# A hybrid state-space layer on one core: the slice softmax in two halves, square sums on GpSimd, and a reordered transpose loop in the last graph layer

## The chip, the cores and the metric

The kernel runs on one core of a Trainium2 chip, as one launch. The metric is the device time of that core in microseconds (us), the median of several runs. The core has five engines that run their own instruction streams in program order and meet through semaphores: TensorE (PE; its weight loads are shown apart as PEld), VectorE (DVE), ScalarE (ACT), GpSimd (POOL) and SyncE (SP), which only issues DMAs here. Matmul results land in PSUM; all other tiles lie in SBUF, 128 partitions wide.

## The reference, cut to what matters

The network has four layers on `x` of shape (128, 40, 128), float32; each layer adds a graph network and a feed-forward network to `x`. Two of these eight blocks are touched.

The feed-forward block of layer 0 assigns the 40 nodes of each graph to 64 slices per head, runs a bidirectional state-space mixer over the slices, and returns to the nodes. Its parts that matter here:

```
w    = softmax(logits / temperature)        # (graph, node, 8 heads, 64 slices)
norm = sum of w over the nodes              # 1 / (norm + 1e-5) scales the slice tokens
...                                         # projection, convolution, scan, gate
yg = yg * rsqrt(mean(yg * yg, -1) + 1e-5) * norm_w      # 512 features
return yg @ out_w.T                         # then back to the nodes with w
```

The graph block of layer 3 is an attention with 8 heads of 40 x 40:

```
logits = q + swapaxes(k, -1, -2)
masked = leaky_relu(logits + (1 - adj) * NEG)
attn   = softmax(masked, axis=-1)
out    = attn @ feat_proj                   # then a projection, a residual, a sigmoid
```

## The kernel before

**Layer 0, feed-forward (`l0_ffn`).** The 128 graphs go in 16 chunks of 8 graphs (`NCH = 16`), each of 4 groups of 2 graphs (`CHP = 4`); of a pair of graphs, one lies on partitions 0 to 39 and the other on 64 to 103. The work is a software pipeline over turns `c = -2 .. 15` (`all_turns`). In one turn each engine does a part of chunk c+2 (logits and softmax), a part of chunk c+1 (slice tokens, input projection, convolution) and the end of chunk c (mixing, gate, norm, output projection, return to the nodes). The order on each engine is written out by hand in its `turn` function, and every engine does exactly what stands there, in that order. A turn on TensorE is: `slices` and `input_projection` of c+1, `mix` of c (L3601), `steps_down` of c+1 (L3571), `logits` of c+2 (L3507, L3508), `gains` of c+1 (L3581, L3583), then

- `output_projection` of group 0 (L3620, 8 matmul records), which waits for the gate (`yg1`),
- `squares` (L3609): four one-column matmuls that average the squared features over the partitions; it waits for `sq_sum`,
- `output_projection` of groups 1 and 2; group q from 2 on waits until ScalarE has copied group q-2 out of the same PSUM bank (`ot_out`),
- `slice_sums` of c+2 (L3519), which waits for the finished softmax (`smd`),
- `output_projection` of group 3, `back_to_nodes` (L3632), `transposed(0)` and `(1)`, `dt_down`, `to_features` (L3642).

The copy of an output group on ScalarE (`out_copy`, L3763) scales by `rms`, which comes from the squares by a chain: Square on ScalarE (L3748), two adds on VectorE that fold four feature blocks into one (`square_sums`, L3897 over 1024 elements and L3899 over 512), `squares` on TensorE, a square root on ScalarE (`root`, L3752), a reciprocal on VectorE (`scales`, L3903).

The softmax of chunk c+2 works in place on the tile `sw` of 128 x 2048 (4 groups of 8 heads of 64 slices). VectorE adds biases to four groups as their logits arrive (`biases`, L3793 into `sw`, L3794 into `fx`), then runs `square_sums(c)`, then the maximum (L3801), the subtraction (L3803, `smx`), `scales(c)`, a wait for one Exp over the whole tile on ScalarE (L3684, `sme`), the sum (L3806), a reciprocal (L3808) and the product (L3810, `smd`). `inverses` (L3815) waits for `slice_sums` of TensorE. Behind it on VectorE stand two pieces of work for a later layer (`kept.piece`, L2481 to L2491), copies for the return (L3908), `out` (L3913), and the states of the next turn (L3827).

On ScalarE a turn ends with `squares`, `root`, `exps(c + 2)`, four `out_copy` and `nodes`. Exp and Sqrt use different tables, so a table load stands before each.

GpSimd has one job in this block: `kept.fetch`, which moves 32 pieces (two in a turn) of an edge list through two buffers: an iota, a wait until VectorE has made the piece (`done`), two DMAs out, a wait for them, and two DMAs in for the piece after the next. All of it stands in one loop.

In the last turns nothing of chunks c+2 or c+1 is left: turn 14 has no logits and no softmax, turn 15 only `mix`, the gate, `squares`, the output projection and the return.

**Layer 3, graph (`l3_gnn`).** 16 chunks of 4 pairs, 64 pairs in all. For each pair TensorE turns the 8 heads of both graphs (16 matmuls of 40 x 40 against the identity, L2279, 32 records), ScalarE copies them to `PT` (L2327), TensorE multiplies them with the features (L2242), ScalarE copies that to `Z` (L2301), and once in a chunk 8 projections follow (L2252), spread over the next chunk's pairs 1 to 3. Graph j = 0 of a pair uses rows and output partitions 0 to 39, j = 1 uses 64 to 103, and each has a PSUM bank of its own. The loop runs over j outside and over the 8 heads inside:

```
for j in range(2):
    for h in range(HD):
        mm = pe.matmul(pst[n % 2][j][rows(j), h, :], P[rows(j), c % 2, h, q, :], g.ident[...], ...)
```

VectorE makes the softmax of the next chunk (L2372 to L2384) around an Exp on ScalarE (L2311), and the sigmoid's end of an earlier one (L2389 to L2400); the first of these waits for the projections. GpSimd adds keys, queries and masks (L2348, L2353: 1280 elements a partition each). The graph block of layer 2 has a similar transpose (L1974), whose loop runs over pairs outside and j inside, 8 matmuls with 16 records in a chunk.

Of the kernel before, what the change touches and what calls it, by code (L numbers as in the profile page):

```python
# [19 lines left out]
NCH = B // CHG  # L20
# [2137 lines left out]
def l3_gnn(nc, g):  # L2158
# [4 lines left out]
    with nc.cleanup_on_exit(), ExitStack() as ctx:  # L2163
# [54 lines left out]
        def _(pe):  # L2218
# [52 lines left out]
            for c in range(NCH):  # L2271
                pe.wait_ge(attn, c + 1)
                for q in range(CHP):
                    n = c * CHP + q
                    if n >= 2:
                        pe.wait_ge(pt_out, n - 1)
                    for j in range(2):
                        for h in range(HD):
                            mm = pe.matmul(pst[n % 2][j][rows(j), h, :], P[rows(j), c % 2, h, q, :], g.ident[rows(j), rows(j)], start=True, stop=True)  # L2279
                    mm.then_inc(pt_ps, 1)  # L2280
                    if q == 1 and c >= 1:
                        project(c - 1, HEADS_AT[q])
                    if n >= 1:
                        product(n - 1)
                    if c < NCH - 3 and q >= 2:
                        query(c + 3, 2 * q - 4)
                        query(c + 3, 2 * q - 3)
                    if q >= 2 and c >= 1:
                        project(c - 1, HEADS_AT[q])
# [143 lines left out]
class EdgeKeys:  # L2433
# [22 lines left out]
    def fetch(self, pool):  # L2456
        W = self.WIDTH
        ends = [self.g.L2_ffn_edge_index[i].rearrange("(p c) -> p c", p=128) for i in range(2)]

        def load(i):  # L2460
            pool.dma_start(self.src[:, i % 2], ends[0][:, i * W:(i + 1) * W]).then_inc(self.ld[i % 2], 16)
            pool.dma_start(self.dst[:, i % 2], ends[1][:, i * W:(i + 1) * W]).then_inc(self.ld[i % 2], 16)

        load(0)
        load(1)
        for i in range(self.PIECES):
            pool.iota(self.place[:], pattern=[[-1, W]], base=-WIDE - i * W % WIDE, channel_multiplier=0, allow_small_or_imprecise_dtypes=True).then_inc(self.io, 1)
            pool.wait_ge(self.done, i + 1)
            pool.dma_start(self.w_dram[:, i * W:(i + 1) * W], self.src[:, i % 2]).then_inc(self.st[i % 2], 16)  # L2469
            pool.dma_start(self.k_dram[:, i * W:(i + 1) * W], self.dst[:, i % 2].bitcast(F32)).then_inc(self.st[i % 2], 16)  # L2470
            if i + 2 < self.PIECES:
                pool.wait_ge(self.st[i % 2], 32 * (i // 2 + 1))
                load(i + 2)
# [741 lines left out]
def l0_ffn(nc, g, kept, sorted_rows):  # L3215


    with nc.cleanup_on_exit(), ExitStack() as ctx:
# [14 lines left out]
        with ExitStack() as first:  # L3233
# [121 lines left out]
            def _(dve):  # L3355
# [22 lines left out]
                for par in range(2):  # L3378
# [29 lines left out]
                                 "g_ps", "w_rdy", "y_ps", "yg1", "sq", "sq_sum", "r_ps", "rt", "rms", "ot_ps", "ot_out", "o_ps", "oT_out", "oT_act", "f_ps", "f_out", "init", "settled")}  # L3408
# [27 lines left out]
        @block.gpsimd  # L3436
        def _(pool):
            sorted_rows.fill(pool, g.x)
            kept.fetch(pool)
# [50 lines left out]
        def _(pe):  # L3490
# [19 lines left out]
            def slice_sums(k):  # L3510

                pe.wait_ge(s["smd"], k + 1)
# [132 lines left out]
            def turn(c, par):  # L3645
# [13 lines left out]
                if there(c):  # L3659
                    output_projection(c, range(1))  # L3660
                    squares(c)
                    output_projection(c, range(1, CHP - 1))
# [15 lines left out]
        def _(act):  # L3678
# [3 lines left out]
            def exps(k):  # L3682
                act.wait_ge(s["smx"], k + 1)
                act.activation(sw[:], sw[:], ACT.Exp).then_inc(s["sme"], 1)  # L3684
# [80 lines left out]
            def turn(c, par):  # L3765
# [5 lines left out]
                if there(c):  # L3771
                    squares(c)
                    root(c)
                if there(c + 2):
                    exps(c + 2)
# [7 lines left out]
        def _(dve):  # L3783
# [5 lines left out]
            def biases(k):  # L3789

                for q in range(CHP):
# [3 lines left out]
                dve.drain()  # L3795

            def softmax(k, meanwhile):

                sw3 = sw[:].rearrange("p q (h n) -> p (q h) n", n=SG)
                bc = sst[:, :, None].broadcast_to([128, CHP * SH_, SG])  # L3800
                dve.tensor_reduce(sst[:], sw3, AX.X, ALU.max)  # L3801
                dve.drain()
                dve.tensor_tensor(sw3, sw3, bc, ALU.subtract).then_inc(s["smx"], 1)  # L3803
                meanwhile()
                dve.wait_ge(s["sme"], k + 1)
                dve.tensor_reduce(sst[:], sw3, AX.X, ALU.add)  # L3806
                dve.drain()
                dve.reciprocal(sst[:], sst[:])  # L3808
                dve.drain()
                dve.tensor_tensor(sw3, sw3, bc, ALU.mult).then_inc(s["smd"], 1)  # L3810
# [84 lines left out]
            def square_sums(k):  # L3895
                dve.wait_ge(s["sq"], k + 1)
                dve.tensor_tensor(sq[:, 0:2], sq[:, 0:2], sq[:, 2:4], ALU.add)  # L3897
                dve.drain()
                dve.tensor_tensor(sq[:, 0], sq[:, 0], sq[:, 1], ALU.add).then_inc(s["sq_sum"], 1)  # L3899

# [28 lines left out]
            def turn(c, par):  # L3929
# [16 lines left out]
                if there(c + 2):  # L3946
                    biases(c + 2)
                if there(c):
                    square_sums(c)
                if there(c + 2):  # L3950
                    softmax(c + 2, lambda: scales(c) if there(c) else None)
                    inverses(c + 2)
                else:
                    scales(c)
# [135 lines left out]
```

## Time and profile before

| what | us |
|---|---|
| runs before: median (lowest, highest) of 3 | 3103.75 (3088.63, 3108.38) |
| the profiled execution | 3108.4 |
| its span from first to last instruction | 3106.7 |
| TensorE busy | 2448.8 (79%) |
| VectorE busy | 2092.8 (67%) |
| ScalarE busy | 1311.9 (42%) |
| GpSimd busy | 729.9 (23%) |

The page of the profile gives these shares, the span in 40 slices of 77.7 us, the costliest groups of instructions and what ended the idle time before them. A timeline view gives instructions in order of time; a run of like instructions is merged into one row. A windows view gives busy times, the number of instructions and the granted TensorE clock (1.00 is the higher of its two levels, 0.50 the lower) in a stretch. Ends of matmuls are modelled, so starts are the safer numbers on TensorE.

### The profile page before, as it was taken

What the parts mean: (1) busy time and instruction counts of PE and PEld (TensorE: products, weight loads), DVE (VectorE), ACT (ScalarE), POOL (GpSimd) and SP (SyncE); (2) the same over time, 40 slices, a digit from 0 to 9 for tenths busy, and PEclk for the clock granted to TensorE, in tenths of its full rate; (3) what the DMA queues carried; (4) which work ended last, traced back from release to release, by engine and by line L of the source; (5) the groups of instructions that cost most, each with busy time, mean ns of one, the idle gap of its engine ahead of it and who ended that gap; (6) DMA issues with size and microseconds to landing.
All of it is one profiled execution on the core that took longest, in us unless ns stands there. A gap on an engine that the chain in (4) does not pass through costs nothing. (4 is left out here: it accounts for less than half of the span.)

```text
span 3106.7 us, 50319 instructions
## 1 busy us (share of the span) xinstructions
PE 2448.8 (79%) x18840; PEld 1551.7 (50%) x18840; DVE 2092.8 (67%) x4114; ACT 1311.9 (42%) x2407; POOL 729.9 (23%) x756
## 2 busy tenths in 40 slices
PE   6467999999999999996567566868758989996291
PEld 5334555545555444553436555634424666664291
DVE  6846888888888878886666797766673356775132
ACT  4334444444444444442457403333214454555171
POOL 0000000000000000001007582047730013440666
PEclk7778999999999999998768857579978997887596
DMA  4341222212222211221323412000012221111263
GB/s 81 114 128 29 53 55 56 55 49 55 56 55 56 56 49 44 57 52 56 101 68 93 79 42 36 8 10 6 6 17 60 68 49 36 44 35 35 75 177 102
DMA packets 189057, 178.78 MB, mean 58 GB/s; under 512 B 83700, under 2 KB 162176, under 8 KB 185976
## 3 DMA queue, kind: packets, MB, share of 16 engines
q1 hardware_dynamic: 168064, 137.00, 17.6%
q0 software_dynamic: 20768, 38.75, 5.2%
q8 instruction: 145, 2.38, 0.3%
q14 instruction: 80, 0.66, 0.1%
HBM read 139.11 MB, written 43.64 MB: 59 GB/s over the span
## 5 line engine op out<-in xcount | busy, mean ns | idle before, releaser
L3557 PE MATMUL hy_ps<-hy_uT,hy_win 128*128 128x512 f32 x1152 | 501.4, 596 | 0.0
L3557 PEld LDWEIGHTS hy_ps<-hy_uT,hy_win 128*128 128x128 f32 x1152 | 218.9, 191 | 286.3 <-issue 286.3
L2469 POOL DMA_DIRECT2D ek_w<-ek_src x32 | 17.8, 556 | 1128.2 <-DVE ek_dst L2491 1128.2
L3620 PE MATMUL hy_ps<-hy_wo,hy_yg 128*128 128x512 f32 x512 | 236.7, 607 | 22.3 <-ACT XNP L3763 15.5
L3055 PE MATMUL er_c<-XNG 128*128 128x400 f32 x480 | 181.0, 534 | 0.0
L3620 PEld LDWEIGHTS hy_ps<-hy_wo,hy_yg 128*128 128x128 f32 x512 | 93.2, 191 | 131.5 <-issue 97.5
L3842 DVE TENSOR_TENSOR_SCAN XNG<-XNG,hy_fx 128x2048 f32<-128x2048 f32 x32 | 141.6, 4425 | 3.0 <-issue 0.4
L2988 POOL DMA_INDIRECT er_gone<-er_nodes,er_sidx x120 | 125.3, 1044 | 36.6 <-issue 35.6
L3055 PEld LDWEIGHTS er_c<-XNG 128*128 128x128 f32 x480 | 95.7, 205 | 68.8 <-issue 12.6
L946 DVE TENSOR_TENSOR f_hg<-f_hs,f_gb 128x640 f32<-128x640 f32 x64 | 52.7, 825 | 110.1 <-ACT f_hs L928 91.3
L2252 PE MATMUL g_ps<-g_Z,g_wc 128*128 128x320 f32 x256 | 106.5, 564 | 1.1 <-ACT g_Z L2301 1.1
L3693 ACT ACTIVATE hy_swT<-hy_ps 64x160 f32<-64x160 f32 x256 | 76.4, 299 | 72.7 <-PE hy_ps L3524 67.9
L2690 PE MATMUL f_px<-XNG 128*128 128x40 bf16 x736 | 69.2, 266 | 47.9 <-DVE XNG L2605 46.7
L1724 POOL DMA_INDIRECT XNP<-f_y,f_pidx x80 | 96.5, 1206 | 42.2 <-issue 24.1
L3793 DVE TENSOR_TENSOR hy_sw<-hy_ps,hy_blg 128x512 f32<-128x512 f32 x64 | 44.3, 692 | 91.2 <-PE hy_ps L3508 91.2
L2279 PEld LDWEIGHTS g_ps<-ident,g_P 40*40 40x40 f32 x2048 | 83.5, 128 | 44.5 <-issue 36.9
L928 ACT ACTIVATE f_hs<-f_ph,f_b1t 128x320 f32<-128x320 f32 x128 | 67.0, 527 | 84.5 <-PE f_ph L896 83.9
L2279 PE MATMUL g_ps<-ident,g_P 40*40 40x40 f32 x2048 | 91.2, 215 | 12.3 <-DVE g_obias L2414 9.5
L3712 ACT ACTIVATE hy_xr<-hy_ps 128x512 f32<-128x512 f32 x80 | 47.9, 599 | 123.9 <-PE hy_ps L3557 123.5
L1710 POOL DMA_INDIRECT f_xg<-f_xn,f_gidx x94 | 91.1, 969 | 28.7 <-issue 27.5
L3763 ACT ACTIVATE XNP<-hy_ps,hy_rms 128x512 f32<-128x512 f32 x64 | 42.2, 682 | 129.2 <-PE hy_ps L3620 128.6
L2690 PEld LDWEIGHTS f_px<-XNG 128*128 128x128 bf16 x736 | 60.7, 152 | 56.4 <-DVE XNG L2605 56.4
(698 smaller groups left out, 5944.7 us busy)
## 6 DMA issues: line engine op xcount, KB each, us to landing
XNG<-hy_decays SPq DMA_DIRECT2D x32, 1024.0 KB, 10.4
hy_rb<-hy_inverse SPq DMA_DIRECT2D x128, 128.0 KB, 3.5
f_gb<-gate_rows SPq DMA_DIRECT2D x16, 640.0 KB, 5.1
g_KB<-g_keys SPq DMA_DIRECT2D x32, 320.0 KB
f_xg<-f_rows SPq DMA_DIRECT2D x54, 128.0 KB
f_ys<-f_ysl SPq DMA_DIRECT2D x54, 128.0 KB
f_y<-f_ysl SPq DMA_DIRECT2D x47, 128.0 KB
f_rows<-in_x_dram POOLq DMA_DIRECT2D x2, 2560.0 KB, 15.6
```

The costliest lines, as they stand in the source:

```text
L928: ins = act.activation(hs[:, e % 2, k, :], psh[e % 2][k][:], ACT.Gelu, bias=b1t[:, e * H2 + k:e * H2 + k + 1])
L1710: pool.indirect_dma_start(out=xg[:, i % NX, h, :], out_offset=None, in_=ex.xn_dram, in_offset=bass.IndirectOffsetOnAxis(ap=ex.gidx[:, n:n ...
L1724: pool.indirect_dma_start(out=yc[:, n % NC_, t, c, :], out_offset=None, in_=ex.y_dram, in_offset=bass.IndirectOffsetOnAxis(ap=ex.pidx[:, n ...
L2252: mm = pe.matmul(psy, wc[:, h, :], Z[:, c % 2, h].rearrange("p b n -> p (b n)"), start=(h == 0), stop=(h == HD - 1))
L2279: mm = pe.matmul(pst[n % 2][j][rows(j), h, :], P[rows(j), c % 2, h, q, :], g.ident[rows(j), rows(j)], start=True, stop=True)
L2690: mm = pe.matmul(self.ph, self.OL[:, b, :, k], self.OH[:, b, :, k], start=False, stop=False, skip_group_check=True)
L2988: pool.indirect_dma_start(out=gone[:, par, u, :], out_offset=None, in_=tab_dram, in_offset=bass.IndirectOffsetOnAxis(ap=sidx[:, par, u:u + ...
L3055: mm = pe.matmul(flat(acc[j][:]), OD[:, 1 - par, u, j * 128:(j + 1) * 128], flat(X[:, u]), start=False, stop=False, skip_group_check=True)
L3557: mm = pe.matmul(p[:], win[:, t, m * 128:(m + 1) * 128], uT[:, t, :], start=(t == 0), stop=(t == KT - 1))
L3620: mm = pe.matmul(PS[4 + q % 2][:], yg[:, t, q * 128:(q + 1) * 128], wo[:, t, :], start=(t == 0), stop=(t == KT - 1))
L3693: ins = act.activation(o, p[:, :, j, 0:N], ACT.Copy)
L3842: dve.tensor_tensor_scan(L[:, a][:, st], dAb[:, a][:, st], E[:, st], 0.0, ALU.mult, ALU.add)
```

## The change

Layer 0: the softmax of a chunk is done in two halves of two groups each. VectorE makes biases, maximum and subtraction of groups 0 and 1, then of groups 2 and 3 (`shifted`), then `scales(c)`, then sum, reciprocal and product of each half (`scaled`). ScalarE runs Exp on the first half, then the root of chunk c, then Exp on the second half. The two adds of the squares move from VectorE to GpSimd. On TensorE `squares(c)` moves in front of the output projection, whose groups 0 to 2 follow it in one stretch. GpSimd's loop over the pieces is opened: the same steps as before, with the square sums of a chunk ahead of its two pieces. `slice_sums` waits for both halves.

Layer 3: the transpose loop runs over heads outside and j inside.

```diff
-                    for j in range(2):
-                        for h in range(HD):
+                    for h in range(HD):
+                        for j in range(2):
                             mm = pe.matmul(pst[n % 2][j][rows(j), h, :], P[rows(j), c % 2, h, q, :], g.ident[rows(j), rows(j)], start=True, stop=True)
...
         def _(pool):
+            def square_sums(k):
+                pool.wait_ge(s["sq"], k + 1)
+                pool.tensor_tensor(sq[:, 0:2], sq[:, 0:2], sq[:, 2:4], ALU.add).then_inc(s["sq_half"], 1)
+                pool.wait_ge(s["sq_half"], k + 1)
+                pool.tensor_tensor(sq[:, 0], sq[:, 0], sq[:, 1], ALU.add).then_inc(s["sq_sum"], 1)
+
             sorted_rows.fill(pool, g.x)
-            kept.fetch(pool)
+            kept.fetch(pool, 0)
+            kept.fetch(pool, 1)
+            for c in range(NCH):
+                square_sums(c)
+                kept.keep(pool, 2 * c)
+                kept.refill(pool, 2 * c)
+                kept.keep(pool, 2 * c + 1)
+                kept.refill(pool, 2 * c + 1)
...
-                pe.wait_ge(s["smd"], k + 1)
+                pe.wait_ge(s["smd"], 2 * k + 2)
...
                 if there(c):
-                    output_projection(c, range(1))
                     squares(c)
-                    output_projection(c, range(1, CHP - 1))
+                    output_projection(c, range(CHP - 1))
                 if there(c + 2):
                     slice_sums(c + 2)
...
-            def exps(k):
-                act.wait_ge(s["smx"], k + 1)
-                act.activation(sw[:], sw[:], ACT.Exp).then_inc(s["sme"], 1)
+            def exps(k, f):
+                act.wait_ge(s["smx"], 2 * k + f + 1)
+                act.activation(sw[:, 2 * f:2 * f + 2], sw[:, 2 * f:2 * f + 2], ACT.Exp).then_inc(s["sme"], 1)
...
                     squares(c)
+                if there(c + 2):
+                    exps(c + 2, 0)
+                if there(c):
                     root(c)
                 if there(c + 2):
-                    exps(c + 2)
+                    exps(c + 2, 1)
...
+            def shifted(k, f):
+
+                for q in range(2 * f, 2 * f + 2):
                     dve.wait_ge(s["lf_ps"], 4 * k + q + 1)
                     dve.tensor_tensor(sw[:, q, :], PS[q % 2][:], blg[:], ALU.add)
                     dve.tensor_tensor(fx[:, q, :], PS[2 + q % 2][:], bfx[:], ALU.add).then_inc(s["lg_out"], 1)
                 dve.drain()
+                sw3, part, wide = half_of(f)
+                dve.tensor_reduce(part, sw3, AX.X, ALU.max)
+                dve.drain()
+                dve.tensor_tensor(sw3, sw3, wide, ALU.subtract).then_inc(s["smx"], 1)
+
+            def scaled(k, f):
+
+                dve.wait_ge(s["sme"], 2 * k + f + 1)
+                sw3, part, wide = half_of(f)
+                dve.tensor_reduce(part, sw3, AX.X, ALU.add)
+                dve.drain()
+                dve.reciprocal(part, part)
+                dve.drain()
+                dve.tensor_tensor(sw3, sw3, wide, ALU.mult).then_inc(s["smd"], 1)
...
                 if there(c + 2):
-                    biases(c + 2)
+                    shifted(c + 2, 0)
+                    shifted(c + 2, 1)
                 if there(c):
-                    square_sums(c)
+                    scales(c)
                 if there(c + 2):
-                    softmax(c + 2, lambda: scales(c) if there(c) else None)
+                    scaled(c + 2, 0)
+                    scaled(c + 2, 1)
                     inverses(c + 2)
-                else:
-                    scales(c)
```

## Rows read from the trace of the kernel before

**Rows 1.** Windows view: layer 0 feed-forward between its ends; layer 3 graph
```profile
core 0: us, PE busy (x) PEld busy (x) DVE busy (x) ACT busy (x) POOL busy (x), PEclk, DMA share, GB/s
...
255.00:1397.00 1142.00, 1066.71 (x9282) 568.91 (x9282) 918.15 (x1183) 543.24 (x949) 67.98 (x140) 0.99 0.21 52
...
2567.00:2824.00 257.00, 253.89 (x2648) 172.08 (x2648) 174.48 (x160) 128.41 (x284) 89.82 (x28) 0.82 0.14 35
```
**Rows 2.** Timeline of PE, one turn (start us, us, instruction [idle before <-releaser])
```profile
708.91 3.68 PE L3620 MATMUL hy_ps<-hy_wo,hy_yg 128*128 128x512 f32 x8
...
713.23 3.68 PE L3620 MATMUL hy_ps<-hy_wo,hy_yg 128*128 128x512 f32 x8
717.99 3.70 PE L3620 MATMUL hy_ps<-hy_wo,hy_yg 128*128 128x512 f32 x8 [1.08 <-ACT XNP L3763]
722.53 1.08 PE L3519 MATMUL hy_ps<-hy_sw,hy_selS 128*32 128x128 f32 x32 [0.84 <-DVE hy_sw L3810]
...
737.88 1.92 PE L3560 MATMUL hy_ps<-hy_uT,hy_wdt 128*40 128x512 f32 x8 [1.84 <-DVE hy_uT L3827]
```
**Rows 3.** Timeline of DVE, the same turn
```profile
704.66 0.68 DVE L3794 TENSOR_TENSOR hy_fx<-hy_ps,hy_bfx 128x512 f32<-128x512 f32 x1
...
708.87 1.22 DVE L3897 TENSOR_TENSOR hy_uT<-hy_uT 128x1024 f32<-128x1024 f32 x1
...
710.78 2.28 DVE L3801 TENSOR_REDUCE hy_sst<-hy_sw 128x32 f32<-128x2048 f32 x1
...
717.40 2.29 DVE L3806 TENSOR_REDUCE hy_sst<-hy_sw 128x32 f32<-128x2048 f32 x1 [1.89 <-ACT hy_sw L3684]
...
720.18 2.29 DVE L3810 TENSOR_TENSOR hy_sw<-hy_sw,hy_sst 128x2048 f32<-128x2048 f32 x1
```
**Rows 4.** Timeline of ACT, the same turn
```profile
701.55 1.92 ACT L3748 ACTIVATE hy_uT<-hy_yg 128x2048 f32<-128x2048 f32 x1
...
713.69 1.28 ACT L3684 ACT_TABLE_LOAD   x1
715.46 1.91 ACT L3684 ACTIVATE hy_sw<-hy_sw 128x2048 f32<-128x2048 f32 x1 [0.48 <-DVE hy_sw L3803]
```
**Rows 5.** Tile views of layer 3's keys and attention (min/median/max ns)
```profile
L2348 POOL TENSOR_TENSOR g_KB<-g_KB,g_Q x16: 2390/2392/2397, 2550.9 to 2782.7; 128x1280 f32<-128x1280 f32 x16
L2353 POOL TENSOR_TENSOR g_KB<-g_KB,a_adjG x16: 2882/4024/4032, 2553.3 to 2785.2; 128x1280 f32<-128x1280 f32 x16
...
L2378 DVE TENSOR_TENSOR g_P<-g_P,g_st x16: 1491/2257/2264, 2559.4 to 2798.4; 128x1280 f32<-128x1280 f32 x16
```
**Rows 6.** Timeline of PE: first softmax, and the last two turns
```profile
182.97 1.93 PE L3519 MATMUL hy_ps<-hy_sw,hy_selS 128*32 128x128 f32 x32 [13.28 <-DVE hy_sw L3810]
...
1398.22 3.70 PE L3620 MATMUL hy_ps<-hy_wo,hy_yg 128*128 128x512 f32 x8
...
1402.56 10.55 PE L3620 MATMUL hy_ps<-hy_wo,hy_yg 128*128 128x512 f32 x24
...
1442.37 5.30 PE L3620 MATMUL hy_ps<-hy_wo,hy_yg 128*128 128x512 f32 x8 [6.80 <-DVE hy_yg L3892]
```
**Rows 7.** Timeline of ACT, turn 14: the Square
```profile
1397.29 1.92 ACT L3748 ACTIVATE hy_uT<-hy_yg 128x2048 f32<-128x2048 f32 x1
```
**Rows 8.** Timeline of PE: turned heads in layer 2, and twice in layer 3
```profile
1939.83 0.50 PE L1974 MATMUL g_t<-ident,g_P 40*40 40x40 f32 x16
...
2649.25 1.29 PE L2279 MATMUL g_ps<-ident,g_P 40*40 40x40 f32 x32 [0.44 <-DVE g_P L2384]
...
2687.20 2.11 PE L2279 MATMUL g_ps<-ident,g_P 40*40 40x40 f32 x32
```
**Rows 9.** Timeline of DVE in layer 3: the same step of two successive chunks
```profile
2635.22 0.55 DVE L2389 SCALAR_TENSOR_TENSOR g_so<-g_ps,g_obias,XNP 128x320 f32<-128x320 f32 x1 [0.34 <-PE g_ps L2252]
...
2649.11 0.55 DVE L2389 SCALAR_TENSOR_TENSOR g_so<-g_ps,g_obias,XNP 128x320 f32<-128x320 f32 x1
```
**Rows 10.** Windows view: one chunk of layer 3, mostly at the low clock
```profile
2581.00:2603.00 22.00, 21.88 (x170) 14.68 (x171) 8.63 (x8) 7.67 (x17) 6.40 (x2) 0.58 0.13 31
```

More of the change, by code:

```diff
@@ L2454, in hold, with fetch, keep, refill @@
         self.ld = [sem(f"ld{b}") for b in range(2)]
-    def fetch(self, pool):
+    def fetch(self, pool, i):
         W = self.WIDTH
[L2458 to L2473, printed above, removed]
+        cols = slice(i * W, (i + 1) * W)
+        for t, end in ((self.src, 0), (self.dst, 1)):
+            rows_ = self.g.L2_ffn_edge_index[end].rearrange("(p c) -> p c", p=128)
+            pool.dma_start(t[:, i % 2], rows_[:, cols]).then_inc(self.ld[i % 2], 16)
+    def keep(self, pool, i):
+        W = self.WIDTH
+        pool.iota(self.place[:], pattern=[[-1, W]], base=-WIDE - i * W % WIDE, channel_multiplier=0, allow_small_or_imprecise_dtypes=True).then_inc(self.io, 1)
+        pool.wait_ge(self.done, i + 1)
+        pool.dma_start(self.w_dram[:, i * W:(i + 1) * W], self.src[:, i % 2]).then_inc(self.st[i % 2], 16)
+        pool.dma_start(self.k_dram[:, i * W:(i + 1) * W], self.dst[:, i % 2].bitcast(F32)).then_inc(self.st[i % 2], 16)
+    def refill(self, pool, i):
+        if i + 2 < self.PIECES:
+            pool.wait_ge(self.st[i % 2], 32 * (i // 2 + 1))
+            self.fetch(pool, i + 2)
     def piece(self, dve, i):
@@ L3407, in l0_ffn @@
                                  "ip_ps", "ip_out", "dt_half", "dt_sum", "cv", "xs", "dtln", "dt_rdy", "da_exp", "da_rdy", "da_ld", "xt_ps", "xt_out",
-                                 "g_ps", "w_rdy", "y_ps", "yg1", "sq", "sq_sum", "r_ps", "rt", "rms", "ot_ps", "ot_out", "o_ps", "oT_out", "oT_act", "f_ps", "f_out", "init", "settled")}
+                                 "g_ps", "w_rdy", "y_ps", "yg1", "sq", "sq_half", "sq_sum", "r_ps", "rt", "rms", "ot_ps", "ot_out", "o_ps", "oT_out", "oT_act", "f_ps", "f_out", "init", "settled")}
         da_st = [sem(f"da_st{i}") for i in range(2)]
@@ L3787, in _, with half_of @@
             dve.nop().then_inc(s["f_out"], 2)
-            def biases(k):
-                for q in range(CHP):
+            def half_of(f):
+                part = sst[:, f * 2 * SH_:(f + 1) * 2 * SH_]
+                return sw[:, 2 * f:2 * f + 2].rearrange("p q (h n) -> p (q h) n", n=SG), part, part[:, :, None].broadcast_to([128, 2 * SH_, SG])
+            def shifted(k, f):
+                for q in range(2 * f, 2 * f + 2):
                     dve.wait_ge(s["lf_ps"], 4 * k + q + 1)
@@ L3795, in biases @@
                 dve.drain()
[L3797 to L3801, printed above, removed]
+                sw3, part, wide = half_of(f)
+                dve.tensor_reduce(part, sw3, AX.X, ALU.max)
                 dve.drain()
[L3803 to L3806, printed above, removed]
+                dve.tensor_tensor(sw3, sw3, wide, ALU.subtract).then_inc(s["smx"], 1)
[3 more added lines that the diff above has]
+                dve.tensor_reduce(part, sw3, AX.X, ALU.add)
                 dve.drain()
-                dve.reciprocal(sst[:], sst[:])
+                dve.reciprocal(part, part)
                 dve.drain()
-                dve.tensor_tensor(sw3, sw3, bc, ALU.mult).then_inc(s["smd"], 1)
+                dve.tensor_tensor(sw3, sw3, wide, ALU.mult).then_inc(s["smd"], 1)
             def inverses(k):
@@ L3893, in gate @@
                 ins.then_inc(s["yg1"], 1)
[L3895 to L3899, printed above, removed]
             def scales(k):
```

## The prediction

> **What bounds the kernel now.** I read the windows view by stage first, then the timelines of the engines through one turn. In the inner part of layer 0's feed-forward block TensorE is busy for 1066.71 of 1142 us at a granted clock of 0.99, VectorE for 918.15 [rows 1]. So TensorE sets the end there, and an edit pays only if it takes away one of TensorE's waits. In layer 3's graph block TensorE is busy for 253.89 of 257 us, at a clock of 0.82, VectorE for 174.48 [rows 1]: TensorE again, but with a clock that comes and goes.
>
> The timeline of one turn shows where TensorE waits in the stretch that the change rewrites. An output group of 8 records lasts 3.68 us alone and three in a row last 10.55 [rows 2, 6], so an unhindered group puts off its successor by (10.55 - 3.68) / 2 = 3.43 us. From group 1 to group 2 there are 717.99 - 713.23 = 4.76 us: 1.33 too many, spent on the copy of group 0, which waits for the root. From group 2 to the slice sums there are 722.53 - 717.99 = 4.54: 1.11 too many, spent on the softmax [rows 2]. The idle figures at those rows, 1.08 and 0.84, are smaller because modelled ends overlap the next start; I go by starts. That is 2.44 us in a turn. Both waits need a softmax and square sums in the same turn, which turns 0 to 13 have: 14 turns, 34.2 us.
>
> **Do both waits go?** I lay out the turn of rows 2 to 4 anew. TensorE reaches the squares at 708.91, where group 0 starts now. Group 0, squares and the start of group 1 take 4.32 us, so the squares take 0.89; then group 0 starts at 709.8, group 1 at 713.2, group 2 at 716.7, and the slice sums could start at 720.1.
>
> *Square sums on GpSimd.* Square ends on ScalarE at 701.55 + 1.92 = 703.5 [rows 4]. No row shows such an add on GpSimd here; the nearest are its adds of 1280 elements: 2.39 with a broadcast operand, 2.88 at the least and 4.02 in the median with a full one [rows 5]. For 1024 plus 512 elements, 1.2 times as many, that is 2.9 to 4.8 us. I take 3.5, from the 2.88, since these operands are full. The sums are ready at 707.0, at the latest 708.3, and TensorE wants them at 708.9: no wait. The queue in front on GpSimd is last turn's pieces, and GpSimd is busy for 67.98 of 1142 us [rows 1]. Behind the new wait stand the iota and the DMAs of this turn's pieces; VectorE wants them only after the slice sums, some 13 us later. All of the pieces' DMAs keep their number and their distance to the piece that releases them. SP's queue isn't touched.
>
> The add's 2.88 became 4.02 where a subtraction of VectorE with two SBUF operands ran beside it, and that subtraction went from 1.49 to 2.26 [rows 5]: one waits for the other. The Trainium skill, "SBUF — State Buffer", section "SBUF: two separate sides", says that the two engines hold a shared port exclusively for a whole instruction, which speaks against an add on GpSimd beside a softmax. By that rule the first half's subtraction waits for the end of the second add, at most about half a microsecond, and the sum stays as it is; the trace agrees in size.
>
> *Softmax in halves.* The second operation of group 1 ends at 705.34, unchanged [rows 3]. An operation over 1024 elements costs 1.22 us [rows 3] and 0.08 for the drain; half of the 2.29 of a full one, 1.15, is the lower bound. Maximum and subtraction of the first half end at 707.9. Groups 2 and 3 are four operations of 0.68: 710.7. Their maximum and subtraction: 713.3, and the reciprocal of the root, a short one: 713.5. Each half then needs a sum, a reciprocal with its drains and a product: 1.22 + 0.49 + 1.22 = 2.9, where 0.49 is the gap from 717.40 + 2.29 to 720.18 [rows 3]. The second product ends at 719.4 instead of 722.47. What went: 1.9 us of adds from 708.87 to 710.78, and the 1.89 of waiting for Exp [rows 3]; half an Exp now runs beside the other half's work. TensorE comes at 720.1, so the margin is 0.7 us, or 1.5 with the lower bound, or 0.2 if the port costs half a microsecond. Each tenth that is missed costs 1.4 us in 14 turns.
>
> *Root between the Exps.* ScalarE pays a table load more in each turn, 1.28 us [rows 4]. First Exp: 707.9 to 708.9 (half of 1.91). Table: 710.2. Root, whose squares are done at 709.9: 710.5. Table: 711.8. It then waits for the second half until 713.3 anyway, so the load is hidden. Second Exp: 714.3; copy of group 0 until 715.0. Group 2 needs that copy at 716.7: 1.7 us to spare, and beyond these the load would cost its own length.
>
> Everything behind the slice sums (inverses, their DMAs, the pieces, states) hangs on them or on TensorE's later work, so the ring follows as a whole: a turn of 34.2 / 14 = 2.44 us less.
>
> **The ends of the pipeline.** The first two turns have a softmax and nothing beside it; TensorE waits 13.28 us for the first [rows 6]. The wait for Exp goes there too: 2 x 1.9 = 3.8 us won. Turn 14 has no logits that cover the squares: Square ends at 1399.21 [rows 7], GpSimd at 1402.7, and TensorE stands from 1398.22 [rows 6], where it now does group 0: 4.5 us lost. In turn 15 the gate ends at 1442.3, Square takes 1.9 and GpSimd 3.5, so the squares start at 1447.8. Today group 0 runs beneath that (5.3 us at the low clock [rows 6]); it then comes after: 5.5 us lost, bounds 3.4 and 7. Layer 0: 34.2 + 3.8 - 4.5 - 5.5 = 28 us won.
>
> **The loop in layer 3.** 16 records with j inside last 0.50 us in layer 2, 32 with j outside last 1.29 [rows 8], both at the high clock. If records of the two graphs overlap, 32 cost some 0.78 (0.50 and 16 more at 0.28), so 0.5 us in each of 64 groups: 32 us at most at the high clock. Against this stands VectorE: its step L2389 comes 13.89 us after the one before in a chunk in which it hardly waits (0.34), and TensorE then waits for it (0.44) [rows 8, 9]. A chunk can't fall below 13.9, and the mean is 257 / 16 = 16.1 [rows 1]. The excess lies in chunks with the clock down, as the one of 22.0 at 0.58 [rows 10], where a group costs 2.11 [rows 8]. Chunks at the floor gain nothing, the others 2 us and more. I take 15 of the 32. Bounds: 30 won, and below nothing, in the rival on the clock.
>
> **The sum.** 28 + 15 = 43 us. The profiled execution took 3108.4 (span 3106.7 and 1.7 around it): 3065.4. It lies 4.65 above the median shown, so 3061 for the median.
>
> **The rivals.**
> *Layer 3 gives nothing* (VectorE's floor, or no overlap of records): for it the 0.44 wait [rows 8]; against it the 0.50 of layer 2. 28 us: 3076. The same time comes out if the halves are late and the wait for the softmax, 1.11 a turn, stays.
> *Layer 0 gives the time back.* TensorE waits 1.84 us for the states before the input projection [rows 2]; if VectorE's states don't move up, this wait grows by 2.44 and only the ends are left: 3.8 - 10 = -6, and 15 from layer 3: 3095. Against it: VectorE is released by the slice sums themselves.
> *The clock of layer 3 falls, and the whole is slower.* With shorter groups TensorE waits about 2 us in each chunk for VectorE. If that brings the low clock for the whole stage, a chunk costs the 22.0 of rows 10 less about 0.9 in each of four groups, 18.4, and 16 of them 294 us: 37 more than now, less 28 from layer 0: 3113. It decides from a mean chunk of 16.1 + 28 / 16 = 17.8 us. For it: the clock of 0.82 in a stage in which TensorE hardly waits [rows 1]; against it: in the low chunk of rows 10 TensorE is busy for 21.88 of 22.00 us, so it wasn't waiting that brought the clock down there. The Trainium skill, "TensorE: Matmul & The Clock Gate", section "HAM oscillation", warns that small gaps between groups of matmuls bring the clock down; [rows 10] show a low clock without a gap of that kind.
>
> **How the numbers follow.** Chances: forecast 0.60, layer 3 without a gain 0.20, layer 0 giving back 0.13, low clock 0.07. A measurement here can tell about 1% from no change, 31 us. The forecast lies 43 below; a part of it, and little of the first rival, falls on either side of 3073: faster 0.64, within 1% 0.33, slower 0.03. Range 3040 (all bounds good: 34 from layer 0, 30 from layer 3) to 3095 (the third case): what is left out is the low clock and some of the third.
>
> **What would show it.** A turn of 74.4 us; TensorE without idle time before groups 2 and the slice sums; L3519 about 11.2 us after the first squares; the two GpSimd adds together 3 to 4.8 us and done before TensorE comes; a new wait at L3609 in turns 14 and 15 alone. In layer 3 groups under 0.9 us at the high clock, a stage of some 242 us, more waits for L2384. Wrong: a squares wait in each turn, slice sums later than 720.1 on this scale, or L2279 groups still above 1.2 us.

## The result, and the profile after

Median 3074.64 us over 7 runs (3068.62 to 3077.12), beside 3101.85 for the kernel before over 7 runs (3084.28 to 3108.38): a ratio of 0.9919, 95% interval 0.9893 to 0.9945. That is 27 us faster, inside the range; the forecast said 43. The profiled execution took 3077.12 us (span 3075.4), 31.3 less than the one before.

The end is near; the way to it isn't the one that was forecast. Cutting both traces at the same instructions gives, in us:

| stretch | before | after | gain | forecast |
|---|---|---|---|---|
| layer 0, first logits to the last projection to features | 1301.9 | 1301.1 | 0.8 | 28 |
| layer 3's turned heads, L2279 first to last | 254.0 | 225.2 | 28.8 | 15 |
| everything else | | | 1.7 | 0 |

Layer 0, where the change has all of its parts but one, gained nothing in this pair of profiles. The 1.7 is a sum of -6.3 ahead of layer 0's block, 9.2 between the two stretches and -1.2 at the end, where nothing was edited: single profiles differ by that much. The windows view of the changed kernel, over the stretches of [rows 1]:

```profile
core 0: us, PE busy (x) PEld busy (x) DVE busy (x) ACT busy (x) POOL busy (x), PEclk, DMA share, GB/s
255.00:1397.00 1142.00, 1083.93 (x9302) 578.31 (x9303) 906.75 (x1235) 570.66 (x981) 121.74 (x171) 0.96 0.21 53
2563.00:2789.00 226.00, 206.36 (x2640) 132.00 (x2640) 173.31 (x159) 123.56 (x280) 89.86 (x28) 0.87 0.16 39
```

In layer 0 TensorE is busy for longer than before, 1083.93 us instead of 1066.71, at a granted clock of 0.96 instead of 0.99: the waits went, and slower matmuls took their place. In layer 3 it went the other way: fewer busy microseconds and a higher clock.

The turn itself came out as laid out. The timelines of all engines through a turn without a low clock, in order of time:

```profile
705.59 2.35 POOL L3440 TENSOR_TENSOR hy_uT<-hy_uT 128x1024 f32<-128x1024 f32 x1 [39.86 <-ACT hy_uT L3760]
708.02 1.27 POOL L3442 TENSOR_TENSOR hy_uT<-hy_uT 128x512 f32<-128x512 f32 x1
708.76 1.61 DVE L3818 TENSOR_TENSOR hy_sw<-hy_sw,hy_sst 128x1024 f32<-128x1024 f32 x1
710.94 1.03 PE L3622 MATMUL hy_ps<-mean_w,hy_uT 128*128 128x1 f32 x8
711.83 10.55 PE L3633 MATMUL hy_ps<-hy_wo,hy_yg 128*128 128x512 f32 x24
712.78 0.26 ACT L3764 ACTIVATE hy_rms<-hy_ps,eps 128x4 f32<-128x4 f32 x1
714.15 1.22 DVE L3818 TENSOR_TENSOR hy_sw<-hy_sw,hy_sst 128x1024 f32<-128x1024 f32 x1
719.72 1.23 DVE L3828 TENSOR_TENSOR hy_sw<-hy_sw,hy_sst 128x1024 f32<-128x1024 f32 x1
722.31 1.08 PE L3532 MATMUL hy_ps<-hy_sw,hy_selS 128*32 128x128 f32 x32
737.37 1.92 PE L3573 MATMUL hy_ps<-hy_uT,hy_wdt 128*40 128x512 f32 x8 [1.55 <-DVE hy_uT L3845]
```

The three groups of [rows 2] have become one row of 10.55 us with no wait in it or behind it. Such turns last 74.4 to 74.5 us, where those before lasted 76.4 to 77.0.

But only some turns are like that. TensorE's timeline in the next turn:

```profile
783.75 0.68 PE L3594 MATMUL hy_ps<-hy_Cs,hy_xs 64*64 64x64 f32 x16
784.36 1.06 PE L3596 MATMUL hy_ps<-hy_wfd,hy_xs 128*128 128x8 f32 x8
785.28 1.03 PE L3622 MATMUL hy_ps<-mean_w,hy_uT 128*128 128x1 f32 x8
786.17 12.24 PE L3633 MATMUL hy_ps<-hy_wo,hy_yg 128*128 128x512 f32 x24
```

The same 24 records last 12.24 us instead of 10.55. The windows view (columns as above) around the start of these groups, and of the same groups in the turn before:

```profile
712.00:715.00 3.00, 3.00 (x8) 1.33 (x8) 2.83 (x4) 2.31 (x3) 0.00 (x0) 1.00 0.00 0
782.90:786.30 3.40, 3.40 (x36) 2.57 (x35) 3.33 (x5) 1.53 (x2) 0.92 (x2) 1.00 0.03 5
786.30:789.70 3.40, 3.40 (x6) 1.34 (x6) 3.24 (x5) 2.35 (x3) 0.00 (x0) 0.51 0.00 0
```

TensorE has no idle time by its records (3.40 of 3.40), yet the clock is at 1.00, the high level of 2.4 GHz, up to the groups and at 0.51, the low one of 1.2 GHz, right behind their start. What stood ahead of the fall is a row of small matmuls: the gains (L3594, L3596) and now the squares too, 2.4 us together. A window of 3 us behind the start of the groups is well below 1.00 in 7 of the turns 0 to 13, and in none of the kernel before. Another 5 low stretches begin elsewhere in the turn, behind transposes, slices or the wait before the input projection, where TensorE did have idle time just before; before there were 3 of that kind. One stretch costs a turn about 1.75 us: turns with one last 76.0 to 76.7, which is most of what the waits had given.

The last two turns, TensorE's timeline:

```profile
1394.04 1.87 PE L3622 MATMUL hy_ps<-mean_w,hy_uT 128*128 128x1 f32 x8 [4.74 <-POOL hy_uT L3442]
1395.77 16.45 PE L3633 MATMUL hy_ps<-hy_wo,hy_yg 128*128 128x512 f32 x32
1447.18 1.86 PE L3622 MATMUL hy_ps<-mean_w,hy_uT 128*128 128x1 f32 x8 [12.43 <-POOL hy_uT L3442]
1448.90 15.48 PE L3633 MATMUL hy_ps<-hy_wo,hy_yg 128*128 128x512 f32 x32
```

Here the squares do wait for GpSimd, and behind the wait they last 1.87 instead of 1.03 and the groups 16.45 instead of about 14.0. So from the projection to features of turn 0 to that of turn 13 the trace goes from 1004.5 to 990.3 us (14.2 won, where 13 turns of 2.44 are 31.7), and from turn 13 to turn 15 from 111.8 to 128.2 (16.4 lost, where 10 were expected).

Layer 3: the timelines of TensorE and VectorE in two successive chunks, to be held against [rows 8, 9]:

```profile
2602.84 0.55 DVE L2389 SCALAR_TENSOR_TENSOR g_so<-g_ps,g_obias,XNP 128x320 f32<-128x320 f32 x1
2602.87 0.81 PE L2279 MATMUL g_ps<-ident,g_P 40*40 40x40 f32 x32
2616.73 0.55 DVE L2389 SCALAR_TENSOR_TENSOR g_so<-g_ps,g_obias,XNP 128x320 f32<-128x320 f32 x1
2616.87 0.81 PE L2279 MATMUL g_ps<-ident,g_P 40*40 40x40 f32 x32 [1.52 <-DVE g_P L2384]
```

A group of 32 records takes 0.81 us instead of 1.29, TensorE now waits 1.52 us for VectorE, and VectorE's step comes 13.89 us after the last one, the very distance of [rows 9]. The idle time before L2279 that L2384 ends rose from 8.8 us in 12 waits to 31.1 in 22; the view counts matmuls and weight loads together, and for the matmuls alone it is 2.9 us in 5 waits and 12.3 in 9.

### The profile page after: what moved, and what is told of

Read it like the earlier page. It is cut to its first block and busy times, and to the rows that moved or that the text cites. A ratio compares the mean times of both kernels' runs of the same rounds, so it can differ in the third digit from the quotient of the medians.

```text
span 3075.4 us, 50462 instructions
## 1 busy us (share of the span) xinstructions
PE 2427.9 (79%) x18840; PEld 1527.6 (50%) x18840; DVE 2073.6 (67%) x4162; ACT 1330.0 (43%) x2437; POOL 782.2 (25%) x788
## 5 line engine op out<-in xcount | busy, mean ns | idle before, releaser
L3633 PE MATMUL hy_ps<-hy_wo,hy_yg 128*128 128x512 f32 x512 | 243.3, 632 | 0.0
L3440 POOL TENSOR_TENSOR hy_uT<-hy_uT 128x1024 f32<-128x1024 f32 x16 | 37.6, 2353 | 731.1 <-ACT hy_uT L3760 731.1
L3633 PEld LDWEIGHTS hy_ps<-hy_wo,hy_yg 128*128 128x128 f32 x512 | 100.6, 201 | 121.1 <-issue 121.1
L2252 PE MATMUL g_ps<-g_Z,g_wc 128*128 128x320 f32 x256 | 95.2, 514 | 4.4 <-ACT g_Z L2301 4.4
L1390 POOL DMA_INDIRECT f_rows<-XNG,f_pidx x80 | 76.8, 960 | 48.6 <-issue 23.8
L1548 POOL DMA_INDIRECT XNP<-f_ys,f_pidx x80 | 77.7, 972 | 38.7 <-issue 23.8
```

Source lines behind the costliest of these rows:

```text
L1390: pool.indirect_dma_start(out=self.x_dram[h], out_offset=bass.IndirectOffsetOnAxis(ap=self.pidx[:, t, c:c + 1], axis=0), in_=self.xn[:, t, ...
L1548: pool.indirect_dma_start(out=yc[:, n % NC_, t, c, :], out_offset=None, in_=ex.y_dram[n // (PARTS // ex.HALVES)], in_offset=bass.IndirectO ...
L2252: mm = pe.matmul(psy, wc[:, h, :], Z[:, c % 2, h].rearrange("p b n -> p (b n)"), start=(h == 0), stop=(h == HD - 1))
L3633: mm = pe.matmul(PS[4 + q % 2][:], yg[:, t, q * 128:(q + 1) * 128], wo[:, t, :], start=(t == 0), stop=(t == KT - 1))
```

## The experiments

Two theories stood after the result. Mine: in layer 0 the squares, put right behind the gains, make one row of small matmuls behind which the clock falls, and that eats what the removed waits gave. The rival: the falls belong to the shorter turn, to halves and adds, or to whatever the chip does in a run, and the order of the squares is innocent. Each kernel ran on one chip beside runs of the kernel before, and its ratio is to those; "turns 0 to 13", "13 to 15" and "layer 3" are the stretches used above.

**Squares behind the first group again.** The changed kernel with one line moved:

```diff
 if there(c):
+    output_projection(c, range(1))
     squares(c)
-    output_projection(c, range(CHP - 1))
+    output_projection(c, range(1, CHP - 1))
```

> The changed kernel with one edit: squares(c) stands behind output group 0 again, as before the change; halves, root between the Exps, adds on GpSimd and the layer 3 loop stay. Theory (order and clock): in the changed kernel 7 of the low-clock stretches in layer 0's inner part begin right after a run of small matmuls (gains, then squares), and turns 14 and 15 wait for GpSimd with nothing beneath. With a dense group between gains and squares these 7 go (some 1.7 us each, 12 in all), and turns 13 to 15 take some 112 us from one to_features to the last instead of 128; the time falls by about 27 to 3047, with a turn still 74.4 us at the full clock. Rival (chance of phase): the low stretches come back elsewhere in the same number, only the 16 us of the ends are won: 3058. Second rival (root too late): the copy of group 0 waits for the root again, 1.3 us in each turn: 3065 or more.

Measured: 3047.24 us, ratio 0.9821 [0.9775, 0.9867]. Turns 0 to 13 take 976.6 us, 13 to 15 113.9, and none of the 14 windows behind the squares is below 1.00. TensorE's timeline, one inner turn and turn 14:

```profile
703.24 0.95 PE L3622 MATMUL hy_ps<-mean_w,hy_uT 128*128 128x1 f32 x8
704.05 7.14 PE L3633 MATMUL hy_ps<-hy_wo,hy_yg 128*128 128x512 f32 x16
711.12 1.08 PE L3532 MATMUL hy_ps<-hy_sw,hy_selS 128*32 128x128 f32 x32
...
1374.18 1.05 PE L3622 MATMUL hy_ps<-mean_w,hy_uT 128*128 128x1 f32 x8 [1.11 <-POOL hy_uT L3442]
1375.10 10.55 PE L3633 MATMUL hy_ps<-hy_wo,hy_yg 128*128 128x512 f32 x24
```

The move of the squares alone cost the change about as much as it kept: with group 0 between the gains and the squares both waits of [rows 2] are still gone, and in turn 14 the group covers most of the wait for GpSimd. Run again:

> The kernel of e1_squares_back again, beside e12 on the same chip, to tell the two apart. Theory (the place of the two adds doesn't matter once the squares stand behind group 0): 3043 to 3057, within 6 us of e12. Rival (GpSimd's adds carry something): e12 slower by 7 us or more.

Measured: 3049.36 us, 0.9808 [0.9774, 0.9842]; turns 0 to 13 977.4, 13 to 15 114.1. In all seven profiles with a group ahead of the squares, those further down included, none of the 14 windows is low.

**The same instructions in another order.** That run also took the ends' cost away, so the clock's part was taken apart: squares stay ahead of all groups, but the gains go ahead of the logits.

```diff
-if there(c + 2):
-    logits(c + 2)
 if there(c + 1):
     gains(c + 1)
+if there(c + 2):
+    logits(c + 2)
```

> The changed kernel with one edit: gains(c+1) stand ahead of logits(c+2) on TensorE, so that 16 dense records lie between the gains and the squares; no work is added or left out. Theory (small matmuls in one run bring the clock down): the 7 low stretches that follow gains and squares go, 8 to 14 us are won: 3061 to 3067; turns 14 and 15, which have no logits, stay as slow. Rival (the clock falls for another reason, as the shorter turn's phase): as many low stretches as now, 3074.

Measured: 3062.79 us, 0.9867 [0.9822, 0.9911]. Turns 0 to 13 take 977.0 us, as with the squares back, and 13 to 15 take 127.3, as in the changed kernel, where no logits are left to stand between. None of the 14 windows is low. The windows view behind the squares of the same turn as in the disturbed one above:

```profile
773.60:776.60 3.00, 3.00 (x8) 1.33 (x8) 2.91 (x5) 2.95 (x4) 0.00 (x0) 1.00 0.00 0
```

The instructions, their number and the squares' place before the groups are those of the changed kernel; only what stands between gains and squares differs. That the change's parts or the shorter turn bring the falls is out.

**The row made longer.** Each of the squares' matmuls is done twice, which adds about 1 us to the row.

```diff
-for q in range(CHP):
+for q in list(range(CHP)) * 2:
```

> The changed kernel with each of the four squares matmuls issued twice (same operands, same output): the run of small matmuls from the gains on grows from 2.4 to 3.3 us, at the suspected place and nowhere else. Theory (a run of small matmuls brings the clock down): besides 16 times 0.9 us of work (14), the low stretches that follow gains and squares go from 7 to 11 or more, 7 us or more: 3095 or above. Rival (their number has to do with phase alone): 7 of them as now, 3089.

Measured: 3102.36 us, 0.9999 [0.9973, 1.0025]. The profile, of the slowest of its ten executions (3116.68), shows 1025.2 us for turns 0 to 13: 78.1 to 80.7 for a turn with a low window, 75.2 and 75.7 for the two without. 12 of the 14 windows are low instead of 7. Two low ones and one of the two that stayed up:

```profile
404.50:407.50 3.00, 3.00 (x4) 1.34 (x5) 2.92 (x4) 2.12 (x3) 0.00 (x0) 0.50 0.00 0
800.80:803.80 3.00, 3.00 (x4) 1.25 (x5) 2.92 (x4) 2.28 (x3) 0.00 (x0) 0.55 0.00 0
1272.70:1275.70 3.00, 3.00 (x8) 1.33 (x8) 2.93 (x4) 2.03 (x3) 0.00 (x0) 1.00 0.00 0
```

Of the 34.9 us over the changed kernel's turns some 13 are the added matmuls themselves (13 turns of 1 us); the rest goes with the clock, for low stretches number 19 instead of 12. A microsecond more of small matmuls in a turn took back the whole gain.

**Each half of the change alone.** The kernel before with only layer 3's new loop:

```diff
-for j in range(2):
-    for h in range(HD):
+for h in range(HD):
+    for j in range(2):
```

> The kernel before with the layer 3 loop alone. Theory: layer 3 is all that the change won; the stage (first turned head to last) takes about 225 us instead of 254 and the time falls by 28 to about 3074, as the whole change does. Rival (the two stages share the gain as predicted, 15 here): 3087. Rival (clock of layer 3 falls without the shifted start): no gain.

Measured: 3086.94 us, 0.9932 [0.9902, 0.9962]; layer 3 230.5 us. Its turns 0 to 13 take 1010.4 us, 6 more than before with not a line of them changed: 5 low stretches of the second kind instead of 3. And the changed kernel with the old loop (the same lines, the other way):

> The changed kernel with the old loop in layer 3: layer 0's part alone. Theory: the 34 us that the two waits cost are given back by the clock (some 17 us in the inner turns) and the last turns (16 us): the time is that of the kernel before, within 5 us, 3097 to 3104. Rival (as predicted, 28 won here): 3074.

Measured: 3090.93 us, 0.9958 [0.9932, 0.9984]; turns 0 to 13 986.6 with 7 of 14 windows low again, 13 to 15 128.5, layer 3 241.2. By times layer 0's half is worth 0.4% and the loop 0.7%, but the profile doesn't bear out the first: of its 22 us against the one before, layer 0 has 4.2 (1301.9 to 1297.7), and 12.8 stand in layer 3, where not a line differs; the rest lies in other stages without an edit. The windows view of that stage:

```profile
2557.20:2798.40 241.20, 237.97 (x2638) 163.30 (x2638) 173.10 (x156) 126.41 (x279) 89.80 (x28) 0.87 0.15 37
```

With the old loop, too, the clock can be 0.87 there, where the trace of before has 0.82. So that stage's time moves with the clock without any edit.

The 241.2 lies between the 254.0 of before and the new loop's stages, so the loop was tried once more on the kernel with the squares back (the same lines again):

> The kernel of e1_squares_back with the old loop in layer 3 (j outside): what layer 0's part is worth once the squares stand behind group 0, and one more sample of the old loop at another phase of the clock. Theory: the stage of layer 3 takes 240 to 255 us (seen so far: 254.0 and 241.2 with the old loop, 224.0 to 230.5 with the new one), the whole 12 to 28 more than e1_squares_back: 3060 to 3075. Rival (the loop is worth little once layer 0 is mended): under 3055.

Measured: 3069.7 us, 0.9871 [0.9829, 0.9913]; layer 3 252.7. On the same chip the kernel with the new loop, the repeat above, took 3049.36: 20 us for the loop.

**What the halves carry.** On the kernel with the squares back the softmax is whole again, with one Exp, the root ahead of it; the adds stay on GpSimd:

```diff
-if there(c + 2):
-    exps(c + 2, 0)
-if there(c):
     root(c)
 if there(c + 2):
-    exps(c + 2, 1)
+    exps(c + 2)
...
-    shifted(c + 2, 0)
-    shifted(c + 2, 1)
-if there(c):
-    scales(c)
+    biases(c + 2)
 if there(c + 2):
-    scaled(c + 2, 0)
-    scaled(c + 2, 1)
+    softmax(c + 2, lambda: scales(c) if there(c) else None)
...
```

> The kernel of e1_squares_back with the softmax in one piece again (one Exp, root ahead of it); adds on GpSimd and the layer 3 loop stay. Theory (the halves take both waits away, the adds on GpSimd little): the waits before group 2 and before the slice sums are back with 1 to 2 us a turn together, and 4 us in the first two turns; a turn of 75.5 to 76.5 us, 3065 to 3075. Rival (the adds on GpSimd are what made the softmax early enough): a turn under 75 us, 3050.

Measured: 3068.34 us, 0.9902 [0.9869, 0.9935]; turns of 76.0 to 77.0 us (78.4 and 80.4 for the two with the clock down), turns 0 to 13 999.1, 22 more than with halves. Its waits, from the source view of the slice sums and VectorE's timeline in one turn:

```profile
  DVE hy_sw L3823: 86.4, 32
```

```profile
712.43 2.29 DVE L3819 TENSOR_REDUCE hy_sst<-hy_sw 128x32 f32<-128x2048 f32 x1 [3.04 <-ACT hy_sw L3697]
715.22 2.29 DVE L3823 TENSOR_TENSOR hy_sw<-hy_sw,hy_sst 128x2048 f32<-128x2048 f32 x1
```

VectorE waits 3.04 us for the one Exp, and the slice sums wait for its product for each of the 16 chunks (32 waits, as the view counts a matmul and its weight load apart); with halves the view has 4, those of the first two turns.

**What GpSimd carries.** On the kernel with the squares back the two adds return to VectorE, between the halves:

```diff
...
 shifted(c + 2, 0)
+if there(c):
+    square_sums(c)
+if there(c + 2):
     shifted(c + 2, 1)
```

> The kernel of e1_squares_back with the two adds of the squares on VectorE again, between the two halves of the softmax. Theory: VectorE's 2 us come back into a chain with 0.7 us to spare at the slice sums: 0.5 to 1.5 us a turn, 3054 to 3068; the last two turns 1 us shorter. Rival (VectorE has the room): 3047, so GpSimd would carry nothing.

Measured: 3052.41 us, 0.9839 [0.9802, 0.9875]; turns 0 to 13 975.2, 13 to 15 111.7. Again:

> The kernel of e8_adds_on_vector again, beside e11 on the same chip. Theory: as e11, 3043 to 3057, with the last two turns 2 us shorter. Rival: slower than e11 by 7 us or more, some 0.5 us in each turn.

Measured: 3052.27 us, 0.9823 [0.9788, 0.9858], beside 0.9808 with the adds on GpSimd on the same chip: no difference that these runs can tell. With the softmax in halves VectorE has room for the adds.

**Who sets the end in layer 3.** On the kernel with the squares back VectorE does the maximum of layer 3's softmax twice:

```diff
 dve.drain()
+dve.tensor_reduce(st[:], p, AX.X, ALU.max)
+dve.drain()
```

> The kernel of e1_squares_back with the maximum of layer 3's softmax (1.49 us on VectorE, once a chunk) done twice, same result. Theory (with the new loop VectorE's ring of 13.9 us is the floor of a chunk): the chunks that now start as soon as the softmax ends (13 of 16 in the changed kernel) grow by 1.55 us each, the stage by 15 to 25 us, 3062 to 3072. Rival (TensorE still sets the stage): 3047 to 3052.

Measured: 3080.09 us, 0.9928 [0.9905, 0.9951]; layer 3 257.5 us, 30 more, or 1.9 in each of 16 chunks for one more operation of about 1.5. The windows view of its layer 3, and the idle time before L2279 that the product (here L2386) ends:

```profile
2538.00:2797.00 259.00, 221.19 (x2641) 140.62 (x2642) 215.63 (x174) 124.94 (x281) 73.96 (x28) 0.79 0.14 34
```

```profile
  DVE g_P L2386: 70.2, 25
```

That is 70.2 us instead of 31.0 without the second maximum (32.0 instead of 12.3 for the matmuls alone), and the stage's clock is 0.79 instead of 0.86. VectorE sets the end there now, and pays for more than the operation. A subtraction of VectorE and GpSimd's second add, in the changed kernel and then here:

```profile
2609.74 2.26 DVE L2378 TENSOR_TENSOR g_P<-g_P,g_st 128x1280 f32<-128x1280 f32 x1
2610.73 4.03 POOL L2353 TENSOR_TENSOR g_KB<-g_KB,a_adjG 128x1280 f32<-128x1280 f32 x1
2726.66 2.89 POOL L2353 TENSOR_TENSOR g_KB<-g_KB,a_adjG 128x1280 f32<-128x1280 f32 x1
2727.23 3.67 DVE L2380 TENSOR_TENSOR g_P<-g_P,g_st 128x1280 f32<-128x1280 f32 x1
```

The second maximum moves the subtraction behind the start of the add. Now it is the subtraction that waits, 3.67 us instead of 2.26, and the add takes 2.89 instead of 4.03. A chunk grows by 1.56 for the operation and by 1.41 for that wait: 13.89 + 2.97 = 16.86, the distance of VectorE's steps in most chunks here. Chunks that were above 13.89 before grow by less, so the mean is 1.9.

The best versions are those with the squares behind the first group: 3047 to 3052 us, 0.981 to 0.984, wherever the adds run.

## Why the prediction was right and wrong

That the total fell into the range is luck: two errors of opposite sign, 27 us too much in layer 0 and, in this pair of profiles, 14 too little in layer 3.

**Do both waits go?** Yes, and nearly by the figures: turns of 74.4 to 74.5 us (74.4 forecast), slice sums 722.31 - 710.94 = 11.4 us behind the squares (11.2), the adds 2.35 + 1.27 = 3.6 us (3.5), done 1.65 us before TensorE comes, the second product 1.36 us before the slice sums (0.7). The first half's subtraction takes 1.61 us where GpSimd's second add runs into it and 1.22 in the second half, as in both with the adds on VectorE: a wait of 0.39, under the half microsecond allowed. The whole softmax shows that the halves carry this term: without them 22 us of the turns come back. The adds on GpSimd were costed rightly and carry none of it that these runs can tell.

**"The ring follows as a whole": the step that failed.** Of 31.7 us in 13 turns, 14.2 showed up. The step took TensorE's durations as given, each at the high clock as in [rows 2]. With the squares moved, a row of small matmuls was formed, and in half of the turns the clock fell behind it; with a group or the logits in between, 7 low windows of 14 became none and 13 turns won 27.1 to 27.9 us (1004.5 less 977.4 to 976.6), so most of the term was sound and the order spoiled it. I had read of the move only that each instruction keeps its length and that no wait comes of it. The rival in which layer 0 gives the time back had the size (3095 us with 15 from layer 3) but by another mechanism: the wait for the states didn't grow, it went from 1.84 to 1.55 in the turns shown. The Trainium skill, "TensorE: Matmul & The Clock Gate", section "HAM oscillation — how this bites in real kernels", ties the low clock to gaps in which TensorE waits between bursts. The ends agree with it: 4.74 us of waiting, then squares at 1.87 instead of 1.03. The inner turns don't: 3.40 us busy of 3.40 stood ahead of the fall.

**The ends.** Waits as worked out (4.74 for the 4.5 of turn 14; in turn 15 12.43 where it was 6.80, so 5.6 for 5.5). What was left out is what the clock does behind them: squares and groups 3.3 us longer in turn 14. 16.4 us lost instead of 10. With one group ahead of the squares the ends cost 2 us. The first two turns gave 3.0 us, which is what 14.2 and 16.4 leave of layer 0's 0.8, for the 3.8 forecast.

**Layer 3's term.** 15 forecast with a bound of 30, 28.8 measured in this pair of profiles. Groups of 0.81 us (forecast under 0.9), the floor of 13.89, and more waits for L2384 came as said. But 12.8 of the 28.8 lie between two profiles of the old loop, 254.0 us at a clock of 0.82 and 241.2 at 0.87; from there to the new loop's 225.2, at 0.87 too, it is 16.0, near the forecast. Three profiles with the old loop show 241.2, 252.7 and 254.0, nine with the new one 224.0 to 230.5, near 16 x 13.89 = 222; the means lie 22 apart. By times the loop is worth 20 to 22 us (on the kernel before and with the squares back), and 12 by the ratios of the changed kernel and of the one with the old loop. So the term was some microseconds too small: what was mis-sized is the share of chunks that could gain, of which I let half stay at the floor. The Trainium skill, same page, part "Packing small matmuls — row/col tiling", says that a weight load overlaps matmuls in flight only if it goes to another row group; the shorter groups agree, and no run here tells load from matmul.

The rival that let the clock fall didn't come true: 0.84 to 0.88 in the nine stages with the new loop. That the shorter groups raise it isn't shown, since the old loop has 0.82, 0.87 and 0.82. The argument against that rival was a misreading all the same. In the chunk of [rows 10] the clock was low from the stage's start, behind a wait of 9.45 us; that TensorE was busy within it doesn't show what had brought the clock down. From the trace of before, a row of TensorE's timeline and windows (columns as above): the start of the stage, and a place where the clock did fall behind groups of turned heads without a wait:

```profile
2567.07 3.14 PE L2279 MATMUL g_ps<-ident,g_P 40*40 40x40 f32 x55 [9.45 <-DVE g_obias L2414]
2567.00:2581.00 14.00, 13.82 (x148) 10.91 (x148) 8.48 (x8) 6.91 (x15) 6.41 (x2) 0.50 0.19 49
2602.70:2606.10 3.40, 3.40 (x70) 2.65 (x69) 2.98 (x4) 2.10 (x5) 0.86 (x1) 1.00 0.00 0
2606.10:2609.50 3.40, 3.40 (x8) 1.81 (x6) 2.81 (x2) 0.86 (x2) 3.32 (x2) 0.51 0.75 198
```

So a fall without a wait stood in that trace already, in layer 3. The warning of small gaps that the prediction takes from the Trainium skill, "TensorE: Matmul & The Clock Gate", stands there in the section "A second HAM failure mode: psum-queue depth-cycling". The second maximum agrees with it: TensorE without work for 37.8 us instead of 19.7 in the stage, the clock at 0.79 instead of 0.86. The change itself doesn't: 3.1 us before and 19.6 after, with 0.82 and 0.87.

**What stays open.** The second kind of low stretch, behind transposes, slices or the input projection's wait, counts 1 to 7 in the runs, 3 and 5 with the same instructions in layer 0. What decides in which turn it comes wasn't tried; at about 1.75 us each it makes some 10 us between profiles, and as much doubt on any small term read from one. Nor was it tried why the row of gains and squares brings the clock down in 7 turns and not in the other 7, or what sets the clock of layer 3's stage, 0.82 or 0.87 with the same instructions.

## What to carry to other kernels

When a step of one-column or otherwise small matmuls is moved on TensorE, look at what becomes its neighbour: if that is another row of small matmuls, keep a dense group between them, and read the granted clock behind it, turn by turn. A step moved up a pipeline is covered in the inner turns and bare in the last ones; leave one independent group ahead of it. Where records go to two row halves of the array, put the loop over the halves innermost. And before a stage's gain is credited to an edit, compare the stage's clock in both traces: here a stage without an edit moved by 12.8 us.

## What the runs showed of the hardware that was not expected

- The clock fell without any idle time of TensorE in its records: 1.00 over 3.40 us that were all busy, 0.51 over the next 3.40. The order of the same instructions decided it: 7 of 14 turns with gains and squares together, 0 of 14 with the logits between. With the squares doubled it was 12 of 14.
- Alternating the row halves shortens 32 records of 40x40 from 1.29 to 0.81 us at the high clock; that took TensorE off the bound of its stage, worth 16 us at the same clock of 0.87.
- The same instructions of a stage took 254.0 us at a clock of 0.82 in one kernel and 241.2 at 0.87 in another that differs only ahead of it.
- One more VectorE operation of about 1.5 us in each of 16 chunks cost 30 us, not 24: it made a subtraction start 0.57 us behind a GpSimd add instead of 0.99 ahead of it, and then the subtraction waited for the add (3.67 us instead of 2.26).
